# Row loads, pair loads and late statistics reordered in an attention and mixture-of-experts layer

## The chip, the core and the metric

The kernel runs on one NeuronCore of a Trainium2 chip. The metric is the device time of one execution, in microseconds; the medians below are over several executions. The core has five engines that run side by side, each with its own instruction queue: TensorE (PE, matmul), VectorE (DVE), ScalarE (ACT), GpSimd (POOL) and SyncE (SP), which here only issues DMA transfers. Semaphores tie them together: an engine that waits holds up everything behind the wait on its own queue.

## What is computed

One transformer layer on 4096 rows of 512 values, all float32:

```python
x = layernorm(x + attention(x))   # 8 heads of 128, window of 128, q and k normalised, gated
x = layernorm(x + ffn(x))
# ffn, for each row:
scores = softmax(x @ gate_w.T)             # 8 experts
weights, idx = top_k(scores, 2)
y = sum over the 2 chosen e of weights[e] * (silu(x @ w1[e].T) * (x @ w3[e].T)) @ w2[e].T
z = (silu(x @ ws1.T) * (x @ ws3.T)) @ ws2.T    # shared expert, every row
out = y + z
```

## The kernel before

Each float32 operand of a matmul is split into a high part and a low part (the rest), and a product is three matmuls: high by high, high by low, low by high. ScalarE makes the high parts, VectorE or GpSimd the low parts.

**First half, to about 1088 us.** 32 tiles of 128 rows go through projection, windowed attention, output projection, the first layer normalisation and the routing. A finished tile of rows is stored by `store_rows` in DRAM twice: in `x2_d`, from which the second half reads, and in `eo_d`, in which everything that a row gets later is added up. The routing writes a small record for each row and choice into the table `slot_d` (`scatter_records`, on POOL's queue).

**Second half.** `NQ` = 103 tiles (index q): 12 tiles of the shared expert on rows 0 to 1535 (`S1` = 12), 71 tiles of the eight experts on gathered rows (`NX` = 71), and 20 tiles of the shared expert on the remaining rows (`FIRST` = 83). Step q of TensorE transposes the rows of tile q+1 (L1135), transposes the product `gg` of tile q-1 (L1170), computes the hidden values of tile q (L1159) and the output of tile q-1 (L1187). Beside it ScalarE makes the high parts and the silu, VectorE the low parts (`split_b` L1474, `turned_low` L1751) and the product (`gate_hidden` L1742). TensorE can't compute an output before `gTl` of `turned_low` is there.

- *Early tiles.* SP's queue loads the rows of shared tiles q into five buffers (`bx`, `bx2`; `load` L491; a buffer is free when TensorE has transposed what it held) and the eight weight blocks of 1 MB (`weights` L487), in between. ScalarE and VectorE split one weight block in each of the steps 3 to 11. In step 9 (`SLOT_Q`) TensorE transposes the slot table (L1421), which POOL's queue reads (`slot_table`, L787) once all records have been scattered (L708). On POOL's queue the outputs of the early shared tiles are added into `eo_d` too (`z_store`, L767), partly ahead of the scatters.
- *Late tiles.* A pair of tiles of rows is combined as: sum of its two stored parts, `ga` and `gb` (loads L573 on SP's queue, the sum by POOL, L825), plus the output of the shared expert. For the pairs of early rows the latter is in `eo_d` already. For pair 6 (`EARLY`) the two outputs are kept in `zs` by ScalarE and added by POOL. For later pairs VectorE adds them out of the accumulator bank (`bank_total`, L1860), one tile per step. Then VectorE takes the statistics (`stats`, L1867 and L1869), POOL computes the factors (`pair_power`, L832 to L837), ScalarE normalises into `oo` (L1092) and SP stores. `ORDER` lists the pairs by the order in which they are combined and `AT` gives the step for each, counted from tile 83. Once the last expert result is in `eo_d`, SP loads six pairs at once, and later pair n+6 in the step of pair n; there are `NB` = 8 buffers. POOL adds pair n+3 in the step of pair n. The last pair is done on VectorE by itself (`finish_stats`, `finish_rows2`), and `finish_stats` waits for the factors of pair 14 (`fnm`).

## Time and profile before

| | us |
|---|---|
| median of 3 runs | 1606.99 |
| lowest, highest | 1604.16, 1607.1 |
| profiled execution | 1604.93 |
| its span | 1602.8 |

| engine | busy us | share |
|---|---|---|
| PE (TensorE matmul) | 1566.6 | 98% |
| DVE | 938.6 | 59% |
| ACT | 718.2 | 45% |
| POOL | 679.5 | 42% |

The engine rows of the page give the time in which an engine executed something. TensorE's share is an average: the places in which it stands idle, and those at which its granted clock is half, have to be looked up in its timeline. DMA carries little in the first half and is close to full from about 1090 us on.

### The profile page before, as it was taken

To read this page: it belongs to the slowest core of one execution; us is meant where nothing else is said; L and a number is where in the kernel's file an instruction comes from. 1 tells how busy PE (TensorE), PEld (TensorE's weight loads), DVE (VectorE), ACT (ScalarE), POOL (GpSimd) and SP (SyncE) were. 2 spreads that over 40 slices of the span, in tenths; PEclk is the share of its full clock that TensorE was granted. 3 is DMA by queue.
4 is the path that set the end of the run, shared out by engine and by line. 5 is a ranking of instruction groups with operands and counts; after the bars stand their busy time and mean duration, and the time that the engine had idled before them with its cause. 6 is when DMAs were issued, how large, how long until landed. Compare 5 with 4: busy or idle time off the path is not lost.

```text
span 1602.8 us, 31930 instructions
## 1 busy us (share of the span) xinstructions
PE 1566.6 (98%) x9650; PEld 1387.0 (87%) x9651; DVE 938.6 (59%) x2565; ACT 718.2 (45%) x1624; POOL 679.5 (42%) x636
## 2 busy tenths in 40 slices
PE   7999999999999999999999999999899999999898
PEld 6899999989999999989999999987778888888786
DVE  5555555655556555665565655657655555555376
ACT  4434333443334433443334333446455555655354
POOL 3323333243333432334324333253355555555375
PEclk9999999999999999999999999999999999999999
DMA  8111111111111111111112111139688888888993
GB/s 288 57 60 62 38 34 34 45 54 33 33 33 60 39 33 33 47 52 33 33 33 65 33 33 33 52 114 219 165 214 223 221 215 226 215 222 216 291 387 124
DMA packets 100960, 176.27 MB, mean 110 GB/s; under 512 B 11742, under 2 KB 28638, under 8 KB 100336
## 3 DMA queue, kind: packets, MB, share of 16 engines
q1 hardware_dynamic: 79360, 134.76, 24.9%
q0 software_dynamic: 20064, 40.86, 13.8%
q8 instruction: 26, 0.43, 0.1%
q10 hardware_dynamic: 1488, 0.04, 0.1%
q14 instruction: 22, 0.18, 0.0%
HBM read 128.04 MB, written 57.02 MB: 115 GB/s over the span
## 4 chain that ended last, share of the span: by engine, by line
PE 89%; DMA 6%; DVE 2%; issue 2%; POOL 1%; ACT 1%; SPq 0%; POOLq 0%; DVEq 0%; ACTq 0%
PE bank L1236 33%; PE bank L1159 14%; PE bank L1334 12%; PE bank L1311 7%; PE bank L1187 7%; PE bank L1285 6%; PE bank L1269 3%; PE bank L1298 3%; PE bank L1135 2%; DMA bx<-x_d 2%; DMA w_raw<-in_w2T 1%; PE bank L1170 1%; DMA passing<-in_wqkvT 1%; DMA gb<-eo_d 1%; DMA bx<-x_d,idxc 1%
## 5 line engine op out<-in xcount | busy, mean ns | idle before, releaser
L1236 PE MATMUL bank<-wh,xh 128*128 128x512 f32 (+2 forms) x896 | 339.1, 378 | 1.6 <-DVE wl L1450 1.5
L1236 PE MATMUL bank<-wl,xh 128*128 128x512 f32 (+2 forms) x896 | 327.6, 366 | 0.0
L1236 PE MATMUL bank<-wh,xl 128*128 128x512 f32 (+2 forms) x896 | 326.9, 365 | 0.0
L723 POOL TENSOR_TENSOR rnorm<-ssmax,nhalf 128x4 f32<-128x4 f32 x128 | 131.8, 1030 | 389.2 <-DVE ssmax L1488 383.9
L1236 PEld LDWEIGHTS bank<-wh,xh 128*128 128x128 f32 x896 | 170.2, 190 | 28.4 <-DVE wl L1450 2.1
L1236 PEld LDWEIGHTS bank<-wh,xl 128*128 128x128 f32 x896 | 170.0, 190 | 28.2
L1236 PEld LDWEIGHTS bank<-wl,xh 128*128 128x128 f32 x896 | 170.5, 190 | 22.3
L908 ACT ACTIVATE sq<-bank 128x512 f32<-128x512 f32 x128 | 75.7, 591 | 169.6 <-PE bank L1236 166.6
L1496 DVE TENSOR_TENSOR qkn<-bank,rnorm 128x512 f32<-128x512 f32 x128 | 88.4, 690 | 107.6 <-POOL rnorm L723 107.6
L1334 PE MATMUL bank<-woh,oh 128*128 128x256 f32 (+1 forms) x512 | 147.8, 289 | 1.0 <-DVE xr L1558 1.0
L1483 DVE TENSOR_REDUCE ssum<-sq 128x4 f32<-128x512 f32 x128 | 87.7, 685 | 103.7 <-ACT sq L908 95.9
L1334 PE MATMUL bank<-wol,oh 128*128 128x256 f32 (+1 forms) x512 | 145.0, 283 | 0.0
L1334 PE MATMUL bank<-woh,ol 128*128 128x256 f32 (+1 forms) x512 | 144.7, 283 | 0.0
L942 ACT ACTIVATE oh<-bank 128x512 fp32r<-128x512 f32 x64 | 38.2, 597 | 237.1 <-PE bank L1311 237.1
L917 ACT ACTIVATE qTh<-bank,qks 128x512 fp32r<-128x512 f32 x64 | 43.9, 686 | 211.6 <-PE bank L1269 211.6
L729 POOL TENSOR_TENSOR pp<-pp,gs 128x1024 f32<-128x1024 f32 x64 | 121.3, 1895 | 38.5 <-DVE gs L1541 38.5
L795 POOL DMA_INDIRECT bx<-x_d,idxc x71 | 81.3, 1145 | 124.2 <-DVE idxc L1845 92.6
L927 ACT ACTIVATE pp<-pp,neg_mx 128x256 f32<-128x256 f32 x256 | 126.8, 498 | 6.8 <-DVE neg_mx L1525 5.4
L1311 PEld LDWEIGHTS bank<-pT,vv 128*128 128x128 f32 x1024 | 122.1, 192 | 5.0 <-issue 2.3
L1311 PE MATMUL bank<-pT,vv 128*128 128x128 f32 x1024 | 124.8, 275 | 1.5 <-DVE wol L1714 1.3
L1546 DVE TENSOR_TENSOR ol<-bank,oh 128x512 fp32r<-128x512 f32 x64 | 44.3, 691 | 138.0 <-ACT oh L942 137.9
L1742 DVE TENSOR_TENSOR gg<-bank,gg 128x256 f32<-128x256 f32 x103 | 43.6, 424 | 127.0 <-ACT gg L1034 127.0
(225 smaller groups left out, 3869.2 us busy)
## 6 DMA issues: line engine op xcount, KB each, us to landing
w_raw<-in_w2T SPq DMA_DIRECT2D x71, 512.0 KB
eo_d<-zero_d SPq DMA_DIRECT2D x36, 256.0 KB, 3.0
xt<-in_xT SPq DMA_DIRECT2D x33, 256.0 KB, 3.2
xr<-in_x SPq DMA_DIRECT2D x32, 256.0 KB, 2.7
x_d<-xr SPq DMA_DIRECT2D x32, 256.0 KB, 2.1
eo_d<-xr SPq DMA_DIRECT2D x32, 256.0 KB, 2.3
w_f<-in_w13T SPq DMA_DIRECT2D x8, 1024.0 KB, 11.7
ga<-eo_d SPq DMA_DIRECT2D x16, 512.0 KB, 6.5
```

The lines of the kernel that those rows point to most:

```text
L723: pool.tensor_tensor(rnorm[:, :], ssmax[:, :], nhalf[:, :], ALU.pow).then_inc(rn_s, 1)
L729: pool.tensor_tensor(pp[:, g * HPG:(g + 1) * HPG, :], pp[:, g * HPG:(g + 1) * HPG, :], gs[:, g * HPG:(g + 1) * HPG].unsqueeze(2).to_broadc ...
L795: pool.indirect_dma_start(out=bx[:, b, :], out_offset=None, in_=x2_d, in_offset=bass.IndirectOffsetOnAxis(idxc[:, b, :], 0)).then_inc(bxg_ ...
L927: ins = act.activation(pp[:, h, :], pp[:, h, :], ACT.Exp, bias=neg_mx[:, h:h + 1], scale=-1.0, accum_out=esum[:, h:h + 1])
L1159: mm = pe.matmul(bank[2 + par][:, :], a[:, par, c, :], b[:, c, :], start=(c == 0 and k == 0), stop=(c == DC - 1 and k == 2))
L1187: mm = pe.matmul(bank[6 + par][:, :], a[:, par, m, :], b[:, m, :], start=(m == 0 and k == 0), stop=(m == IC - 1 and k == 2))
L1236: mm = pe.matmul(b[:, 0:n], a[:, par, c, :], wt[:, c, cols], start=(c == 0 and k == 0), stop=(c == DC - 1 and k == 2))
L1285: mm = pe.matmul(psS[b][:, hh * 2 * P:(hh + 1) * 2 * P], a[:, h, :], w[:, :, h, :], start=(k == 0), stop=(k == 2))
L1311: mm = pe.matmul(psO[:, hh * P:(hh + 1) * P], vv[:, k, g * HPG + hh, :], pT[:, hh, k * P:(k + 1) * P], start=(k == 0), stop=(k == 1))
L1334: mm = pe.matmul(out, a[:, h, :], b[:, h, cols], start=(h == 0 and k == 0), stop=(h == H - 1 and k == 2))
L1483: dve.tensor_reduce(ssum[:, :], sq[:, :].rearrange("p (h d) -> p h d", d=P), AX_X, ALU.add)\
L1496: dve.tensor_tensor(qkn[:, j, :].rearrange("p (h d) -> p h d", d=P), b[:, :].rearrange("p (h d) -> p h d", d=P), rnorm[:, :].unsqueeze(2). ...
```

## The change

- Row tiles 8 to 11 get a place of their own, `bx3`, where the low parts of the second weights will be written later. All of the rows 4 to 11 are loaded in one go when the output projection is done, before the last `store_rows`; the weight blocks 4 to 7 follow it. Load 3 goes ahead of the load of the second shared weights.
- `oo` has four buffers of finished pairs in place of two.
- The outputs of four late tiles, not two, are kept in `zs`; so pairs 6 and 7 are added by POOL and `bank_total` starts with tile 87, not 85. `ORDER` begins with pairs 0, 1, 8 and pair 7 comes late; the pairs are combined in the steps 5 to 20 behind tile 83, without a gap.
- SP loads four pairs at once, with the last two row fours among them, and then pair n+4 in the step of pair n; `NB` is 6.
- In the step of the last tile VectorE does `gate_hidden` before the pair's statistics.

```diff
-NB = 8
+NB = 6
-        zs = sbuf(s3, "zs", [P, 2, D])
+        zs = sbuf(s3, "zs", [P, 4, D])
-        oo = sbuf(s3, "oo", [P, 2, 2, D])
+        oo = sbuf(s3, "oo", [P, 4, 2, D])
...
+        s5 = ExitStack()
+        bx3 = sbuf(s5, "bx3", [P, 4, D])
+        s5.close()
...
-            if q0 >= FIRST + 2:
-                return bank_sum, q0 - FIRST - 1
+            if q0 >= FIRST + 4:
+                return bank_sum, q0 - FIRST - 3
...
-        ORDER = [0, 7, 1, 8, 2, 9, 3, 10, 4, 11, 5, 12, 6, 13, 14, 15]
-        AT = [4, 5, 6, 7, 8, 9, 10, 11, 12, 13, 14, 15, 16, 17, 19, 20]
-        FROM_BANK = EARLY + 1
+        ORDER = [0, 1, 8, 2, 9, 3, 10, 4, 11, 5, 12, 6, 13, 7, 14, 15]
+        AT = list(range(5, 21))
+        FROM_BANK = EARLY + 2
...
+            load(3, 3)
             sp.dma_start(sh2_raw[:, :, :], w2T[E, :, :].rearrange("(c p) n -> p c n", p=P)).then_inc(sh2_in, 16)
-            load(3, 3)
             store_rows(NT - 2, 0)
             weights(1)
             weights(2)
             weights(3)
-            store_rows(NT - 1, 1)
             sp.wait_ge(wo_s, 2 * NT)
             load(4, 4)
+            for q in (5, 6, 7):
+                sp.wait_ge(*place_free(q, q))
+                load(q, q)
+            for q in range(8, S1):
+                load(q, q)
+            store_rows(NT - 1, 1)
+            for e in range(4, E):
+                weights(e)
...
-                if n + 6 < PAIRS:
-                    load_pair(n + 6)
+                if n + 4 < PAIRS:
+                    load_pair(n + 4)
...
-                    for i in range(3):
+                    for i in range(2):
                         load_four(i)
...
-                    for n in range(6):
+                    for n in range(4):
                         load_pair(n)
-                        if n == 3:
-                            load_four(3)
+                        if n >= 2:
+                            load_four(n)
...
-                if ORDER[n] == EARLY:
+                if EARLY <= ORDER[n] < FROM_BANK:
...
-                    if n >= 2:
-                        act.wait_ge(o_out[n % 2], 32 * (n // 2))
+                    if n >= 4:
+                        act.wait_ge(o_out[n % 4], 32 * (n // 4))
...
-                if kind(q0 - 1) == "sh" and q0 - 1 < FIRST + 2:
+                if kind(q0 - 1) == "sh" and q0 - 1 < FIRST + 4:
                     take_shared(q - 1, q0 - 1)
...
+                if q0 == NQ - 1:
+                    gate_hidden(q, q0)
                 if pair_at(q0) is not None:
                     combine(pair_at(q0))
-                if q0 < NQ:
+                if q0 < NQ - 1:
                     gate_hidden(q, q0)
...
-                if FIRST + 2 <= q0 - 1 < NQ - 2:
+                if FIRST + 4 <= q0 - 1 < NQ - 2:
                     bank_total(q0 - 1)
```

## Rows read from the trace of the kernel before

**Rows 1.** TensorE's waits, 1060 to 1603: us in total, times, longest.
```profile
PE bank L1187 <- DVE gTl L1751: 6.9, 3, 5.6
PE bank L1135 <- DMA bx<-x_d: 5.5, 3, 3.1
```

**Rows 2.** TensorE's timeline, early tiles: start us, us, what [idle before, releaser].
```profile
1087.61 0.28 PE L1334 MATMUL bank<-woh,ol 128*128 128x256 f32 x1
...
1096.12 0.66 PE L1135 MATMUL bank<-ident,bx 128*128 128x128 f32 x4 [1.89 <-DMA bx<-x_d]
...
1126.42 0.66 PE L1135 MATMUL bank<-ident,bx 128*128 128x128 f32 x4 [3.06 <-DMA bx<-x_d]
...
1132.87 0.34 PE L1421 MATMUL bank<-ident,slot_t 71*128 71x71 f32 x2
1133.74 0.66 PE L1135 MATMUL bank<-ident,bx 128*128 128x128 f32 x4 [0.53 <-DMA bx<-x_d]
...
1138.58 0.60 PE L1135 MATMUL bank<-ident,bx 128*128 128x128 f32 x4
```

**Rows 3.** Timeline of SP's issuing queue, behind the last stores of rows.
```profile
1092.42 1.54 SPq L491 DMA_DIRECT2D bx<-x_d  x3
```

**Rows 4.** Chain of waits, in order of time, 1060 to 1200: start us, us, what.
```profile
1103.37 30.33 DMA bx<-x_d
```

**Rows 5.** Windows of 2 us: busy us by engine, granted clock, DMA share, GB/s.
```profile
1088.00:1090.00 2.00, 2.00 (x14) 1.74 (x13) 1.79 (x6) 1.25 (x3) 0.25 (x1) 1.00 0.07 28
...
1098.00:1100.00 2.00, 2.00 (x6) 1.52 (x6) 0.54 (x2) 1.98 (x2) 1.69 (x3) 0.50 0.83 314
```

**Rows 6.** POOL's timeline, early tiles: store with accumulation, last scatter, table read.
```profile
1101.11 1.06 POOL L767 DMA_DIRECT2D eo_d<-eo  x1
...
1107.54 0.96 POOL L708 DMA_INDIRECT slot_d<-rec_last,slot_last  x1 [0.30 <-issue]
...
1121.77 1.93 POOL L787 DMA_INDIRECT slot_t<-slot_d,blk_u  x1 [6.57 <-DMA slot_d<-rec_last,slot_last]
```

**Rows 7.** Line L767, accumulating stores of shared outputs: landing times.
```profile
DMA to landing us min/median/max: 4.2/10.8/18.6
```

**Rows 8.** TensorE's timeline, late tiles: the transposes of rows.
```profile
1505.38 0.60 PE L1135 MATMUL bank<-ident,xs 128*128 128x128 f32 x4
...
1510.13 0.60 PE L1135 MATMUL bank<-ident,xs 128*128 128x128 f32 x4
...
1521.99 1.05 PE L1135 MATMUL bank<-ident,xs 128*128 128x128 f32 x4
...
1527.43 0.60 PE L1135 MATMUL bank<-ident,xs 128*128 128x128 f32 x4
```

**Rows 9.** VectorE's timeline, the first sum out of a bank.
```profile
1517.58 0.69 DVE L1860 TENSOR_TENSOR ga<-bank,ga 128x512 f32<-128x512 f32 x1 [7.77 <-POOL ga L825]
```

**Rows 10.** POOL's timeline, second and third pair sum.
```profile
1515.20 2.34 POOL L825 TENSOR_TENSOR ga<-ga,gb 128x1024 f32<-128x1024 f32 x1 [0.25 <-DMA gb<-eo_d]
1517.89 2.35 POOL L825 TENSOR_TENSOR ga<-ga,gb 128x1024 f32<-128x1024 f32 x1 [0.34 <-DMA gb<-eo_d]
```

**Rows 11.** Waits of all engines, 1500 to 1603: ScalarE for the stores.
```profile
ACT oo L1092 <- DMA out<-oo: 2.4, 2, 1.7
```

**Rows 12.** Line L573, the pair loads: landing times.
```profile
DMA to landing us min/median/max: 4.5/7.8/13.1
```

**Rows 13.** VectorE's timeline, the last steps.
```profile
1590.91 0.69 DVE L1867 BATCH_NORM_STATS2 bn<-ga 128x6 f32<-128x512 f32 x1
...
1593.22 0.42 DVE L1742 TENSOR_TENSOR gg<-bank,gg 128x256 f32<-128x256 f32 x1 [0.45 <-ACT gg L1034]
...
1595.86 0.69 DVE L1867 BATCH_NORM_STATS2 bn<-ga 128x6 f32<-128x512 f32 x1
```

**Rows 14.** POOL's timeline, the factors of pair 14.
```profile
1592.86 0.23 POOL L832 TENSOR_SCALAR rs<-mv 128x2 f32<-128x2 f32 x1 [7.02 <-DVE mv L1869]
...
1594.26 0.20 POOL L837 TENSOR_TENSOR nm<-nm,rs 128x2 f32<-128x2 f32 x1
```

More of the change, by code:

```diff
@@ L343, in block_kernel @@
         o_s = sem("o_s")
-        o_out = [sem(f"o_out{i}") for i in range(2)]
+        o_out = [sem(f"o_out{i}") for i in range(4)]
         turns = {e.engine: sem(f"turns{n}") for n, e in enumerate((nc.sync, nc.gpsimd, nc.vector, nc.tensor))}
@@ L414, in place @@
         def place(q0):
+            if 8 <= q0 < S1:
+                return q0
             return (q0 + 2) % 4 if kind(q0) == "ex" else row(q0, q0) % 5 if q0 < FIRST + 4 else q0
@@ L422, in rows_of @@
                 return xs[:, q0 - FIRST - 4, :]
+            if 8 <= q0 < S1:
+                return bx3[:, q0 - 8, :]
             return bx[:, b, :] if b < 4 else bx2[:, b - 4, :]
@@ L429, in landed @@
             if q0 >= FIRST + 4:
-                return xs_in[(q0 - FIRST - 4) // 4], 16
-            return bx_in[place(q0)], 16 * (row(q, q0) // 5 + 1)
+                return xs_in[(q0 - FIRST - 4) // 4], 16 * (S1 - 8) + 16 if q0 >= FIRST + 16 else 16
+            if 8 <= q0 < S1:
+                return xs_in[3], 16 * (S1 - 8)
+            return bx_in[place(q0)], 16 * (sum(1 for p in range(q0 + 1) if place(p) == place(q0) and kind(p) == "sh"))
         def place_free(q, q0):
@@ L489, in load @@
             def load(q, q0):
-                sp.dma_start(rows_of(q0), x2_d[row(q, q0) * P:(row(q, q0) + 1) * P, :]).then_inc(bx_in[place(q0)], 16)
+                sp.dma_start(rows_of(q0), x2_d[row(q, q0) * P:(row(q, q0) + 1) * P, :])\
+                  .then_inc(xs_in[3] if 8 <= q0 < S1 else bx_in[place(q0)], 16)
             def store_rows(w, par):
@@ L587, in store_pair @@
                     sp.wait_ge(*((last_s, k + 1) if n == LAST else (o_s, 2 * n + k + 1)))
-                    sp.dma_start(out[(2 * c + k) * P:(2 * c + k + 1) * P, :], oo[:, n % 2, k, :]).then_inc(o_out[n % 2], 16)
+                    sp.dma_start(out[(2 * c + k) * P:(2 * c + k + 1) * P, :], oo[:, n % 4, k, :]).then_inc(o_out[n % 4], 16)
             def combine(n):
@@ L601, in step @@
                     load_second(q + 1, q0 + 1)
-                for k in ((5, 6) if q0 == 3 else (q0 + 3,)):
-                    if kind(k) == "sh" and k < FIRST + 4:
-                        sp.wait_ge(*place_free(k, k))
-                        load(k, k)
-                if 3 <= q0 < E - 1:
-                    weights(q0 + 1)
+                if FIRST <= q0 + 3 < FIRST + 4:
+                    sp.wait_ge(*place_free(q0 + 3, q0 + 3))
+                    load(q0 + 3, q0 + 3)
                 if q0 == FIRST:
                     sp.wait_ge(h_s, FIRST)
-                    for i in range(3):
+                    for i in range(2):
                         load_four(i)
@@ L624, in _ @@
             for q in o_out:
-                sp.wait_ge(q, 16 * NT // 2)
+                sp.wait_ge(q, 16 * NT // 4)
         @block.gpsimd
@@ L818, in add_pair @@
                 pool.wait_ge(g_in[b], 32 * (n // NB) + 32)
-                if ORDER[n] == EARLY:
+                if EARLY <= ORDER[n] < FROM_BANK:
+                    k = ORDER[n] - EARLY
                     pool.tensor_tensor(ga[:, b, :, :], ga[:, b, :, :], gb[:, b, :, :], ALU.add).then_inc(y_s, 1)
-                    pool.wait_ge(y_s, 1)
-                    pool.wait_ge(res_s2, S1 + 2)
-                    pool.tensor_tensor(ga[:, b, :, :], ga[:, b, :, :], zs[:, :, :], ALU.add).then_inc(gab_s, 1)
+                    pool.wait_ge(y_s, k + 1)
+                    pool.wait_ge(res_s2, S1 + 2 * k + 2)
+                    pool.tensor_tensor(ga[:, b, :, :], ga[:, b, :, :], zs[:, 2 * k:2 * k + 2, :], ALU.add).then_inc(gab_s, 1)
                     return
@@ L1089, in normalise @@
                 for k in range(2):
[L1090 to L1092 removed]
+                    if n >= 4:
+                        act.wait_ge(o_out[n % 4], 32 * (n // 4))
+                    act.activation(oo[:, n % 4, k, :], z_of(n)[:, k, :], ACT.Identity, bias=nm2[:, n % 2, k:k + 1],
                                    scale=rs2[:, n % 2, k:k + 1]).then_inc(o_s, 1)
@@ L1897, in finish_rows2 @@
                 if k == 0:
-                    dve.wait_ge(o_out[b], 32 * (LAST // 2))
-                dve.tensor_scalar(oo[:, b, k, :], z_of(LAST)[:, k, :], mv2[:, b, k, 0:1], rs2[:, b, k:k + 1],
+                    dve.wait_ge(o_out[LAST % 4], 32 * (LAST // 4))
+                dve.tensor_scalar(oo[:, LAST % 4, k, :], z_of(LAST)[:, k, :], mv2[:, b, k, 0:1], rs2[:, b, k:k + 1],
                                   ALU.subtract, ALU.mult).then_inc(last_s, 1)
```

1 line of the change is left out of this document (removed).

## Prediction

> **What bounds the kernel now.** I read the waits of TensorE first. Behind 1060 us, where the second half begins, TensorE waited mainly in two places: 6.9 us for `gTl`, 5.6 of it in one piece, and 5.5 us for rows in `bx`, 3.1 in the longest [rows 1]. Elsewhere it is busy end to end, so a change can only give back these stalls, and what the clock costs behind them. Reading order: waits, then TensorE's own timeline around each wait, then the engine or queue named as the releaser. Times are of the profiled execution (1604.93 us, its span 1602.8).
>
> The undisturbed step of a shared tile is 4.75 us, from transpose to transpose (1505.38 to 1510.13) [rows 8]. The stalls are read against it.
>
> **Early stretch, rows before weight blocks.** TensorE waits for row blocks at 1096.12 (1.89 us), at 1126.42 (3.06) and at 1133.74 (0.53) [rows 2]. The first wait has its cause in SP's order: row block 4 is issued only at 1092.42 [rows 3], behind the stores of the last 128 rows of `x2`, although TensorE's output projection ended at 1087.9 [rows 2]. DMA moved almost nothing from 1088 to 1090 (share 0.07) [rows 5]. The later waits come from SP's queue order: row block 10 was issued at 1103.37 and took 30.33 us, because it stood behind weight blocks [rows 4].
>
> After the change the blocks 4 to 11 are issued from about 1088.1, at some 0.5 us each (1.54 us for three [rows 3]), so until about 1092. The stores and the four weight blocks follow. At its landing time of 3.7 us (1096.12 less 1092.42) block 4 is there at 1091.8, before TensorE asks at 1094.23. So the wait of 1.89 us goes, and with it the half clock behind it: 0.50 in 1098 to 1100 [rows 5]. That is 12 matmuls in which about 1.4 us was lost; I take this from the clock row (some 3 us at half speed give up 1.5). The 3.06 and 0.53 us go too, since blocks 9 to 11 no longer stand behind weights. Counted alone, this is 1.89 + 1.4 + 3.06 + 1.4 + 0.53 = 8.3 us.
>
> **What is late next.** At step 9 TensorE also needs the slot table. Its transposes ran at 1132.87, 0.87 us before the late row block's [rows 2]. That table hangs on another chain, on POOL's queue: the store of tile 0 with accumulation at 1101.11, the last records scattered at 1107.54, the wait for them until 1121.77 (6.57 us of POOL idle), and the read of the table, which reached TensorE 11.1 us later [rows 2, 6]. Rows no longer hold TensorE, so it comes to step 9 at 1123.36 (1126.42 less 3.06) less 3.3, plus one step of 4.9 (4.84 is the one from 1133.74 to 1138.58 [rows 2]): about 1125. The table is not there then. What moves in its chain is little. The store at 1101.11 hangs on POOL's work before it, which the change doesn't touch; only the wait for the last slots, between the store's end at 1102.2 and the first scatter, shrinks, by about 1.2 us. DMA stays busy all the while. So the table comes at 1132.87 - 1.2 = 1131.7, and TensorE stands for some 6.5 us in one piece instead of 3.06 and 0.53. The half clock comes back behind that stall and costs 1.5. The next transposes then stand 0.34 us behind the table's, as they could have in the kernel before (1133.74 less 0.53 is 1133.21), at 1132.0, and the step behind is 4.84 + 1.5 long: 1138.35 against 1138.58. The early part thus gives back 0.2 us, by this sum; I take 0.5. Bounds: -1.1 (chain not earlier at all, clock loss paid) and +4 (chain earlier by the whole of the DMA time won, some 4.4 us between 1088 and 1092.4).
>
> The four late weight blocks stand behind two more row blocks (512 KB) and start up to 4 us earlier; they are wanted one per step until step 10, beyond 1135. The longest landing among the transfers in that queue is about 31 us, begun near 1100; so they are in time, price 0. The place ahead of the weights' low part is free until VectorE writes it in step 12: price 0.
>
> **The move of load 3 ahead of the second shared weights** swaps two neighbours in an idle queue: 0.
>
> **Late stretch: sums and statistics a step later.** The large stall: VectorE waits 7.77 us, until 1517.58, with tile 85's `bank_total` [rows 9], which needs the pair sum POOL began at 1515.20 [rows 10]. Behind it in VectorE's order stand the split and `gTl`, for which TensorE waits 5.6 us. From 1510.13 to 1521.99 it needs 11.86 us where 4.75 are due (7.11 lost), and the next step 5.44 (0.69 lost) [rows 8]; the second is the clock's tail. With some 0.3 us more in the steps behind, where a `gg` came late after ScalarE had waited for a store, that is 8.1 us.
>
> After the change the first `bank_total` is tile 87's. It falls due two steps behind 1510.13, so 9.5 us later, and some 0.3 us into that step: 1519.9. It needs three pair sums; the third began at 1517.89 and takes 2.35, so 1520.25 [rows 10]. It is 0.3 us late, and the result is wanted by TensorE only 3.4 us into the step, 1.1 us behind its usual time. So no stall here.
>
> The next demands: the queue delivers a pair (1 MB) per 2.69 us (1515.20 to 1517.89) [rows 10]. The order is now pairs 0, 1, 2, four row blocks (1 MB), pair 3, four row blocks, pair 4. Pair 4 thus lands at about 1517.8 + 4 x 2.6 = 1528.2, its sum is done at 1530.7, and tile 89's `bank_total` is due at 1529.4: 1.3 us late against 1.15 of slack. I price this at 0.2 us, and the ScalarE and POOL work pushed behind it at another 0.3, no more than ScalarE's late normalising cost in the kernel before. POOL does a pair in some 4 us (2.4 the sum [rows 10], 1.6 the power chain, 1592.86 to 1594.46 [rows 14]), so 0.75 us of each step is left to catch up. The second POOL sum of pairs 6 and 7 (2.4 us each, two steps apart) eats three steps of that; it comes when 1.2 us of slack is left at VectorE: 0.2 us.
>
> **Four buffers of finished rows** take away ScalarE's waits for stores, 2.4 us in two pieces [rows 11]. They are off the path apart from the few tenths counted above.
>
> **Four pairs ahead, six buffers.** A load for pair n+4 is issued about one step before POOL's step n+1, which wants it 10 us later; the median landing is 7.8 us, the longest 13.1 [rows 12]. In the closed loop (load, sum 2.4, power 1.5, normalise 1.5, store issue 1.1, waits 1) of four steps, 19 us, a landing of 11.5 us still fits. Price 0, bound 2.
>
> **The tail.** In step 102 VectorE now does `gate_hidden` (1593.22 to 1593.64) before the statistics of pair 14, which ran from 1590.91 to 1592.8 in the shadow of TensorE [rows 13]. They take 1.86 us and would now run until 1595.5. POOL's power chain followed them from 1592.86 to 1594.46 [rows 14], so it now ends at 1597.15. The last statistics wait for it (`fnm`): they began at 1595.86 [rows 13] and would begin at 1597.2. **Cost 1.3 us** on the path, nothing gained, since `gg` waited for ScalarE there anyway. The last `gTl` is some 0.7 us late too, beside the 1.3 and not added to it.
>
> **Sum.** 8.1 - 0.5 - 0.2 - 1.3 + 0.5 = 6.6 us. On the profiled execution's 1604.93 that is 1598.3; on the median of 1606.99 it is 1600.4. The runs shown spread by 3 us, so I take 1599.3.
>
> **Rivals.**
> 1. *The slot table's chain moves with the rows.* Speaking for it: DMA gets 4.4 us of work done that it did not before, and the table's read ran while SP's queue was still full. The accumulating stores on POOL's queue took up to 18.6 us to land when SP's queue was full and 4.2 at the least [rows 7]. If the queue empties 4 us earlier, the read and the stall end up to 4 us earlier: 1595.5. The Trainium skill, "DMA: Bandwidth & Descriptors", section "Queues, rings and completion order", says that each DMA engine takes turns between the queues that have work, packet by packet; by that rule POOL's transfers are slowed as long as SP's queue holds anything, which fits the two landing times and leaves it open whether the read is caught by the earlier end. Chance 0.2.
> 2. *The late stall isn't removed but halved.* The pair loads land later than in the old trace (two fours of row blocks now stand among them), POOL's sum for tile 89 comes 3 us or more late, and TensorE stands 2 to 3 us and pays 1.5 for the clock. Against: the pieces before pair 2 are unchanged. Time 1603.
>    Chance 0.15.
> 3. *Slower than before.* With six buffers a load waits for a normalised pair two steps back; if landings take 16 us in the steady part, the loop of four steps is 4.5 us too long, and over the ten later pairs (2.5 loops) 11 us are lost, against the 6.6: 1610. It decides from 11.5 us on, and turns the sum over at about 14.5. Longest seen 13.1, under a backlog that the change makes smaller. Chance 0.04.
> 4. *It doesn't do what it says:* the stalls go but return in full at the next wait (table early, pair 9 late): within 0.2%. Chance 0.06.
>
> **Chances.** Forecast 0.55, rivals 0.2, 0.15, 0.04, 0.06. A kernel of this kind can be told from no change beyond about 0.2%, or 3.2 us. Faster 0.84 (the forecast, rival 1, and 0.09 of rival 2, which lies near the edge), same 0.12 (the rest of rival 2, and rival 4), slower 0.04. The range reaches from rival 1's 1595.5, less 1.5 of spread, to rival 2's 1603: 1594 to 1603.5.
>
> **What would show it.** Early: no wait for `bx` rows up to step 12; one wait of 5 to 7 us ahead of the table's transposes; half clock behind it; SP's issues of `bx` in one block from 1088. If the wait ahead of the table is under 3 us, rival 1 holds. Late: no wait for `gTl` above 1 us; first `bank_total` near 1520; ScalarE without waits for stores. Tail: statistics of pair 14 behind the last `gg`, and 1.3 us more from the last `hidden` to the end. I am wrong if TensorE waits anywhere behind 1513 for more than 1.5 us.

## The result, and the profile after

The changed kernel takes 1599.78 us (median of 9 runs, 1597.22 to 1603.11) against 1606.99 of the kernel before (9 runs, 1604.16 to 1610.19). The ratio is 0.9963, with a 95% interval of 0.9953 to 0.9972: about 5.9 us faster, between 4.5 and 7.6. (The two medians lie 7.2 us apart; here and below a gain is read from the ratio.) The forecast was 1599.3, with a range of 1594 to 1603.5.

The profiled execution of the changed kernel took 1603.02 us (span 1601.2), among the slowest of its runs, while that of before (1604.93) is among the fastest of its own. So the two spans differ by only 1.6 us, and the traces have to be read by stretches. The table takes the start of TensorE's transposes of a tile's rows as marks. The stretch of the routed experts holds the same work in both kernels. The stretch from tile 12 to tile 18 (31.20 and 31.13 us) is left out.

| stretch, us | before | after | difference |
|---|---|---|---|
| tile 3 to tile 12 | 55.91 | 56.77 | +0.86 |
| tile 18 to tile 87, the experts | 330.33 | 334.01 | +3.68 |
| tile 87 to tile 102 | 79.48 | 71.29 | -8.19 |
| tile 102 to the end of the span | 17.94 | 20.06 | +2.12 |

Over all the kernels run here the expert stretch took between 329.2 and 334.0 us, whatever was changed around it, and no edit touches what is done in it. The 334.01 is the longest of all. Part of its 3.68 us can be read: behind a wait of 1.87 us for the rows of tile 18 the granted clock falls to 0.50, and the step takes 6.67 us; behind the 1.65 us of the kernel before it stays at 1.00, and the step takes 5.08. The fourteen traces of this document part at this place: the six with half clock there have 331.2 to 334.0 us for the stretch, the eight without 329.2 to 330.9. Leave the stretch out, and the rest sums to -5.2 us, which is near the 5.9 of the timed runs.

**TensorE's waits**, 1060 to 1603, after: us in total, times, longest.

```profile
PE bank L1436 <- DMA slot_t<-slot_d,blk_u: 6.5, 1, 6.5
PE bank L1185 <- DVE gg L1757: 3.2, 4, 1.6
PE bank L1150 <- DMA bx<-x_d,idxc: 2.2, 2, 1.9
PE bank L1202 <- DVE gTl L1766: 1.9, 2, 1.4
```

Both large waits of [rows 1] are gone: no wait for `bx<-x_d` is left and 1.9 us for `gTl`, of which 1.4 is in the very last product. In their place stands one wait of 6.5 us for the slot table, and four for `gg`, 3.2 us together, the longest 1.6.

**TensorE's timeline**, early tiles, after (answers to [rows 2]).

```profile
1094.07 0.60 PE L1150 MATMUL bank<-ident,bx 128*128 128x128 f32 x4
...
1101.38 0.44 PE L1185 MATMUL bank<-ident,gg 128*128 128x128 f32 x2 [1.57 <-DVE gg L1757]
...
1121.27 0.60 PE L1150 MATMUL bank<-ident,bx 128*128 128x128 f32 x4
1132.66 0.52 PE L1436 MATMUL bank<-ident,slot_t 71*128 71x71 f32 x2 [6.48 <-DMA slot_t<-slot_d,blk_u]
1132.97 1.06 PE L1150 MATMUL bank<-ident,bx 128*128 128x128 f32 x4
1139.42 0.60 PE L1150 MATMUL bank<-ident,bx 128*128 128x128 f32 x4
```

The rows are there whenever TensorE turns to them. It reaches the table at 1126.18 (1132.66 less 6.48) and stands. The step from 1132.97 to 1139.42 takes 6.45 us where the same step took 4.84 in [rows 2], so half clock costs 1.61 us here. Windows of 2 us show it (busy us by engine, granted clock, DMA share, GB/s): the granted clock is 0.50, TensorE's lower level of 1.2 GHz, until about 1136.

```profile
1130.00:1132.00 2.00, 0.00 (x0) 0.00 (x0) 0.00 (x0) 0.00 (x0) 0.00 (x0) 0.50 1.07 228
...
1134.00:1136.00 2.00, 2.00 (x8) 1.61 (x7) 1.83 (x8) 1.94 (x3) 0.00 (x0) 0.50 0.27 50
1136.00:1138.00 2.00, 2.00 (x9) 1.66 (x8) 1.35 (x2) 0.74 (x1) 0.00 (x0) 0.87 0.00 0
```

**SP's queue and POOL's timeline**, after (answer to [rows 3] and [rows 6]).

```profile
1087.92 3.67 SPq L500 DMA_DIRECT2D bx<-x_d  x8
...
1093.38 3.67 SPq L496 DMA_DIRECT2D w_f<-in_w13T  x4
```

```profile
1101.11 1.07 POOL L781 DMA_DIRECT2D eo_d<-eo  x1
...
1106.34 0.96 POOL L722 DMA_INDIRECT slot_d<-rec_last,slot_last  x1 [0.30 <-issue]
...
1123.47 1.91 POOL L801 DMA_INDIRECT slot_t<-slot_d,blk_u  x1 [10.23 <-DMA slot_d<-rec_last,slot_last]
```

The eight row blocks go out at 1087.92 and four weight blocks, 4 MB, at 1093.38, all at once. The last scatter of records was issued 1.2 us sooner than before, at 1106.34 against 1107.54, but the wait for it ended 1.7 us later, at 1123.47 against 1121.77. From that scatter to the read 17.1 us pass, against 14.2 before. This isn't yet a difference of the two kernels: the late part alone, which has the loads in their old order, takes 16.2 us (see the experiments).

**TensorE's and VectorE's timelines**, late tiles, after (answer to [rows 8] and [rows 9]).

```profile
1505.09 0.60 PE L1150 MATMUL bank<-ident,bx 128*128 128x128 f32 x4
...
1509.85 0.60 PE L1150 MATMUL bank<-ident,xs 128*128 128x128 f32 x4
...
1514.60 0.60 PE L1150 MATMUL bank<-ident,xs 128*128 128x128 f32 x4
...
1519.35 0.60 PE L1150 MATMUL bank<-ident,xs 128*128 128x128 f32 x4
```

```profile
1524.37 0.69 DVE L1875 TENSOR_TENSOR ga<-bank,ga 128x512 f32<-128x512 f32 x1 [0.59 <-PE bank L1202]
...
1529.13 0.69 DVE L1875 TENSOR_TENSOR ga<-bank,ga 128x512 f32<-128x512 f32 x1 [0.59 <-PE bank L1202]
```

Every step takes 4.75 us. Tile 87's transposes are at 1509.85 here and at 1505.38 in [rows 8], so the late part of this trace lies 4.47 us behind that of before. The first sum out of a bank waits 0.59 us for TensorE, where it waited 7.77 for POOL.

**The last steps**, after: VectorE (answer to [rows 13]), then POOL's factors (answer to [rows 14]).

```profile
1590.47 0.42 DVE L1757 TENSOR_TENSOR gg<-bank,gg 128x256 f32<-128x256 f32 x1 [2.29 <-ACT gg L1049]
1590.81 0.69 DVE L1882 BATCH_NORM_STATS2 bn<-ga 128x6 f32<-128x512 f32 x1
...
1594.43 0.70 DVE L1882 BATCH_NORM_STATS2 bn<-ga 128x6 f32<-128x512 f32 x1 [0.85 <-DVE ga L1875]
```

```profile
1592.75 0.23 POOL L847 TENSOR_SCALAR rs<-mv 128x2 f32<-128x2 f32 x1 [4.55 <-DVE mv L1884]
...
1594.14 0.19 POOL L852 TENSOR_TENSOR nm<-nm,rs 128x2 f32<-128x2 f32 x1
```

The statistics of pair 14 now stand behind the last `gg`; POOL's factors follow them and end at 1594.33, and the next statistics start at 1594.43. The releaser that the profile names for these, `ga L1875`, was done at 1593.58; the wait is POOL's.

### The profile page after: what moved, and what is told of

It reads as the page before. It is cut to its first block, busy times and chain, and to the rows that moved or that the text cites. A ratio compares the mean times of both kernels' runs of the same rounds, so it can differ in the third digit from the quotient of the medians.

```text
span 1601.2 us, 31929 instructions
## 1 busy us (share of the span) xinstructions
PE 1564.6 (98%) x9650; PEld 1384.2 (86%) x9651; DVE 938.9 (59%) x2563; ACT 720.6 (45%) x1626; POOL 680.9 (43%) x637
## 3 DMA queue, kind: packets, MB, share of 16 engines
q1 hardware_dynamic: 79360, 134.76, 25.3%
## 4 chain that ended last, share of the span: by engine, by line
PE 88%; DMA 5%; POOL 2%; DVE 2%; issue 2%; SPq 1%; ACT 1%; POOLq 0%; DVEq 0%; ACTq 0%
PE bank L1251 32%; PE bank L1174 14%; PE bank L1349 12%; PE bank L1326 7%; PE bank L1202 6%; PE bank L1300 6%; PE bank L1284 3%; PE bank L1313 3%; PE bank L1150 2%; DMA w_raw<-in_w2T 1%; PE bank L1185 1%; DMA passing<-in_wqkvT 1%; DMA slot_d<-rec_last,slot_last 1%; DMA slot_t<-slot_d,blk_u 1%; DMA bx<-x_d,idxc 1%
## 6 DMA issues: line engine op xcount, KB each, us to landing
w_f<-in_w13T SPq DMA_DIRECT2D x8, 1024.0 KB, 11.4
```

## Experiments

All ratios are to the kernel before, measured beside it. For runs of one group the interval is some 0.13% to each side, 2 us: the timed runs alone can't tell edits of 1 us apart, and where they can't, the stretches of the traces are used.

| kernel | ratio (95%) | tile 3 to 12 | tile 87 to 102 | to the end |
|---|---|---|---|---|
| before | 1 | 55.91 | 79.48 | 17.94 |
| after | 0.9963 (0.9953, 0.9972) | 56.77 | 71.29 | 20.06 |
| early part alone | 0.9994 (0.9985, 1.0003) | 54.46 | 78.22 | 18.02 |
| late part alone | 0.9961 (0.9947, 0.9974) | 56.10 | 71.30 | 18.97 |
| after, old order of the last step | 0.9956 (0.9943, 0.9970) | 57.33 | 71.31 | 18.96 |
| after, POOL's double sums apart | 0.9965 (0.9952, 0.9979) | 56.34 | 71.30 | 19.08 |
| after, records first | 0.9972 (0.9961, 0.9983) | 54.37 | 71.30 | 20.14 |
| after, two weight blocks held | 0.9958 (0.9945, 0.9971) | 55.55 | 71.30 | 20.11 |
| after, both of these | 0.9941 (0.9929, 0.9953) | 52.39 | 71.30 | 20.15 |
| after, all four edits | 0.9918 (0.9906, 0.9931) | 52.92 | 71.30 | 18.02 |
| after, stores behind the table | 0.9938 (0.9924, 0.9953) | 50.56 | 71.30 | 20.14 |
| the same, weights held | 0.9935 (0.9920, 0.9950) | 50.92 | 71.30 | 20.11 |
| stores behind, both tail edits | 0.9927 (0.9913, 0.9942) | 50.57 | 71.30 | 17.99 |
| the same, weights held | 0.9935 (0.9920, 0.9950) | 51.99 | 71.30 | 18.03 |

### The early part alone

The kernel before, with only the new place and the new order of loads; the late part is the old one.

```
+            if 8 <= q0 < S1:
+                return bx3[:, q0 - 8, :]
...
             load(4, 4)
+            for q in (5, 6, 7):
+                sp.wait_ge(*place_free(q, q))
+                load(q, q)
+            for q in range(8, S1):
+                load(q, q)
+            store_rows(NT - 1, 1)
+            for e in range(4, E):
+                weights(e)
```

> The kernel before with the early part of the change alone: rows 4 to 11 in one go, row tiles 8 to 11 in bx3, the last stores of x2 and weight blocks 4 to 7 behind them. My theory (the slot table's chain takes the place of the rows): no wait for rows, one wait of 5 to 7 us ahead of the table's transposes with the half clock behind it, so nothing is gained: ratio to the kernel before 0.999 to 1.001 (between 1.5 us faster and 1.5 us slower). Rival (rows before weights is a gain in itself, which the changed kernel's profiled execution lost elsewhere): 3 us or more faster, ratio 0.998 or less, and a wait under 3 us ahead of the table.

Measured: 1604.97 us (11 runs), ratio 0.9994 (0.9985 to 1.0003). All the waits for rows are gone, and TensorE's waits from 1086 to 1160 begin so:

```profile
PE bank L1435 <- DMA slot_t<-slot_d,blk_u: 4.2, 1, 4.2
PE bank L1184 <- DVE gg L1756: 1.6, 1, 1.6
```

So more than 5 us of waits for rows went, and the gain left of them is 1.0 us, between -0.5 and 2.4. The early part is close to nothing in time: the table, another chain on another queue, took the place of the rows. Its read was issued 15.9 us behind the last scatter. Of the traces above, four have this order of loads and no other early edit, and their stretch from tile 3 to 12 takes 54.46 to 57.33 us; two have the old order, with 55.91 and 56.10. No gain of the early part can be read from them either.

### The late part alone

The kernel before with the other parts of the change: four tiles in `zs`, four `oo`, the new `ORDER`, four pairs ahead. The early loads and the last step are as they were.

```
-        ORDER = [0, 7, 1, 8, 2, 9, 3, 10, 4, 11, 5, 12, 6, 13, 14, 15]
-        AT = [4, 5, 6, 7, 8, 9, 10, 11, 12, 13, 14, 15, 16, 17, 19, 20]
-        FROM_BANK = EARLY + 1
+        ORDER = [0, 1, 8, 2, 9, 3, 10, 4, 11, 5, 12, 6, 13, 7, 14, 15]
+        AT = list(range(5, 21))
+        FROM_BANK = EARLY + 2
...
-                if FIRST + 2 <= q0 - 1 < NQ - 2:
+                if FIRST + 4 <= q0 - 1 < NQ - 2:
                     bank_total(q0 - 1)
```

> The kernel before with the late part alone (sums out of a bank from tile 87, statistics a step later, four pairs ahead, six pair buffers, four buffers of finished rows), and gate_hidden behind the statistics in the last step, as before. My theory: the whole gain is here, 8.2 us from the transposes of tile 88 to those of tile 102, about 1 us lost again in step 101; 7.0 us faster, ratio 0.9955. Rival (both parts gain): 3 to 5 us faster, ratio 0.997 to 0.998.

Measured: 1598.32 us (5 runs), ratio 0.9961 (0.9947 to 0.9974), some 6.3 us. The 15 steps behind tile 87 take 71.30 us, as in the whole change. The end is 18.97 long, 1.0 more than before, although the last step has its old order: this 1.0 us belongs to the late part itself. Which of the late edits the 8 us hang on (the later first sum out of a bank, the order, the four buffers) was not tried one by one; that VectorE's wait for POOL is gone, the trace above shows. In the early part TensorE waits for rows again, 6.7 us in three pieces, the longest 5.1. The two parts taken together give 0.9955, which the whole change (0.9963) matches within its interval.

### The old order in the last step

From here on every edit is one of the changed kernel.

```
-                if q0 == NQ - 1:
-                    gate_hidden(q, q0)
                 if pair_at(q0) is not None:
                     combine(pair_at(q0))
-                if q0 < NQ - 1:
+                if q0 < NQ:
                     gate_hidden(q, q0)
```

> The changed kernel with the last step's order as before (statistics of pair 14 ahead of gate_hidden). My theory: the statistics go back into the shadow of TensorE's work, and 1.2 us of the end are given back: the time from the last transposes of rows to the end of the span is 18.9 us against 20.1; ratio to the kernel before 0.9955 where the changed kernel has 0.9963. Rival (in the new order the late gate_hidden of step 102 would be held up by the statistics, and that is why the end is not longer by the move): same or slower than the changed kernel, ratio 0.9963 or more.

Measured: 1598.03 us, ratio 0.9956 (0.9943 to 0.9970). In the trace the end is 1.10 us shorter (18.96 against 20.06), and 1.06 when the sums of the next edit are spread in both (18.02 against 19.08). The time agrees in sign, but its interval holds that of the change, so it is the trace that shows this one.

### POOL's double sums apart

Pairs 6 and 7 are each summed twice on POOL, 2.40 us a sum. In `ORDER` they come two steps apart and late; here they come in the eighth and twelfth place.

```
-        ORDER = [0, 1, 8, 2, 9, 3, 10, 4, 11, 5, 12, 6, 13, 7, 14, 15]
+        ORDER = [0, 1, 8, 2, 9, 3, 10, 6, 11, 4, 12, 7, 13, 5, 14, 15]
```

> The changed kernel with pairs 6 and 7 at places 7 and 11 of the order in place of 11 and 13, so that GpSimd's two additional sums lie four steps apart and end sooner. My theory: the 0.75 us wait for gg in step 101 and the 1 us that this step is long go, as GpSimd has caught up by then; 1.0 us faster than the changed kernel, ratio to the kernel before 0.9957. Rival (the loss in step 101 comes from DMA or ScalarE and not from GpSimd's backlog): the wait stays, ratio 0.9963.

Measured: 1598.98 us, ratio 0.9965 (0.9952 to 0.9979), no difference from the changed kernel that the timed runs could tell, and not the 0.9957 expected. In the trace the end is 0.98 us shorter. What goes is this chain in the changed kernel (timelines of POOL, ScalarE and TensorE):

```profile
1576.08 2.40 POOL L838 TENSOR_TENSOR ga<-ga,zs 128x1024 f32<-128x1024 f32 x1
```

```profile
1580.19 1.52 ACT L1107 ACTIVATE oo<-ga,nm,rs 128x512 f32<-128x512 f32 x2 [2.29 <-POOL nm L852]
```

```profile
1582.49 0.44 PE L1185 MATMUL bank<-ident,gg 128*128 128x128 f32 x2 [0.75 <-DVE gg L1757]
```

The second sum of pair 7 pushes POOL's factors back, ScalarE waits 2.29 us for them with the next `gg` behind, and TensorE stands 0.75 us. With the sums spread, the only wait of TensorE from 1560 on is the one of 1.43 us in the last product.

### What makes the slot table late

Three theories stood after this. Ahead of the last scatters on GpSimd's queue goes the accumulating store of tile 0; on SP's queue there are four weight blocks; or the scatter needs this time by itself. The first two edits take away one of the causes each, the third both.

`records_first`:

```
             table_constants()
-            z_store(0, 0)
             scatter_records(NG - 1, range(G))
+            z_store(0, 0)
             z_store(1, 1)
```

> The changed kernel with the last records' scatters ahead of the accumulating store of tile 0 on GpSimd's queue. Theory A (the records stand behind that store in GpSimd's queue, which takes 18.6 to 18.9 us to land): the records land 8 us or so earlier, the table's read is issued near 1114 instead of 1123.5, TensorE's wait ahead of it falls from 6.5 us to under 1, with the half clock behind it: 6 to 8 us faster than the changed kernel, ratio to the kernel before 0.9915 to 0.9925. Rival B (the records are slow because the DMA engines are shared with SP's weight blocks and row loads): the records go out 1.4 us earlier and land as long after as before; the wait falls to some 5 us, 1 to 1.5 us faster than the changed kernel, ratio 0.9955.

`weights_held`:

```
             for e in range(4, E):
+                if e == 6:
+                    sp.wait_ge(scat, 16 * NSC)
                 weights(e)
```

> The changed kernel with SP holding back weight blocks 6 and 7 (2 MB) until all records have landed. Theory A (the store of tile 0 ahead of them): little changes, wait ahead of the table 5 us or more, ratio to the kernel before 0.996. Rival B (the weight blocks' traffic): once blocks 4 and 5 are through, near 1106, the records have the engines to themselves and land before 1114; the table's read takes about 5 us beside 2 MB of weights or 9 at most; TensorE waits under 1 us, and 6 to 8 us are gained, ratio 0.9915 to 0.9925. If the held blocks come too late, TensorE waits at the first expert tile instead.

`both_table` has the two together.

> The changed kernel with both edits: records ahead of the store of tile 0, and weight blocks 6 and 7 held until the records have landed. Both theories: the wait ahead of the table is gone; 6.5 us of wait and 1.6 of half clock less what the next wait (the gathered rows of the first expert tile, 0.4 before) takes back: ratio to the kernel before 0.9915. If neither edit alone does it and this one does, the records need both.

Measured, with the chain in its two halves: from the issue of the last scatter to that of the table's read, from POOL's timelines, and from there to the table's transposes. Where TensorE doesn't wait, the second half is an upper bound.

| kernel | time, us | ratio | scatter to read | read to transposes | together | wait for the table |
|---|---|---|---|---|---|---|
| before | 1607.39 | 1 | 14.2 | at most 11.1 | at most 25.3 | none |
| after | 1599.78 | 0.9963 | 17.1 | 9.2 | 26.3 | 6.5 |
| early part alone | 1604.97 | 0.9994 | 15.9 | 8.2 | 24.1 | 4.2 |
| old order of the last step | 1598.03 | 0.9956 | 15.9 | 10.3 | 26.2 | 6.3 |
| double sums apart | 1598.98 | 0.9965 | 16.3 | 8.6 | 24.9 | 5.1 |
| records first | 1601.87 (10 runs) | 0.9972 | 12.8 | 11.4 | 24.2 | 3.9 |
| weights held | 1601.12 | 0.9958 | 13.3 | 10.8 | 24.1 | 4.3 |
| both | 1598.39 | 0.9941 | 11.0 | 11.0 | 22.1 | 1.9 |

The 1607.39 is of the kernel before beside the last three; the other rows had their own beside them, so times are compared by the ratio. The four kernels with the change's chain (rows two to five) show how far one execution lies from another: 15.9 to 17.1 us in the first half, 24.1 to 26.3 together. With the old order of loads the first half took 14.2 us in one trace and 16.2 in the other (the late part alone), so that the change made it longer is not shown.

Each edit takes 3 to 4 us off the first half, and neither the 6 to 8 that its theory wanted. The second half, 11.4 and 10.8 us, is longer than in any of those four and gives most of it back; why was not tried. The whole chain, 24.2 and 24.1 us, lies at the lower end of the four, and the waits for the table, 3.9 and 4.3 us, beside the 4.2 of the early part alone. The timed runs agree: 0.9972 and 0.9958 are no gain on 0.9963, and the first is worse than either of its theories expected. Only the two edits together shorten the whole chain clearly, to 22.1 us (22.7 in the kernel with all four edits). `both_table` is the first kernel that the timed runs set apart from the change (0.9929 to 0.9953 against 0.9953 to 0.9972, touching), at 0.9941 and not the 0.9915 expected. In all three the clock's loss stays: behind 3.90, 4.26 and 1.85 us of waiting the steps take 6.36, 7.47 and 6.41 us, where 4.84 are due.

```profile
1129.96 0.50 PE L1438 MATMUL bank<-ident,slot_t 71*128 71x71 f32 x2 [1.85 <-DMA slot_t<-slot_d,blk_u]
1130.25 1.06 PE L1152 MATMUL bank<-ident,bx 128*128 128x128 f32 x4
1136.66 0.60 PE L1152 MATMUL bank<-ident,bx 128*128 128x128 f32 x4
```

With both edits, a window of the 12 us from 1106 on shows what is left: the two weight blocks that were not held were issued by 1097.1 and took at most 13.2 us to land, the DMA engines are still nearly full, and yet they move little. Before it the same stretch of the change; the last two columns are DMA share and GB/s.

```profile
1106.00:1118.00 12.00, 11.41 (x58) 8.98 (x57) 11.39 (x24) 8.39 (x14) 4.61 (x6) 1.00 1.12 170
```

```profile
1106.00:1118.00 12.00, 11.12 (x55) 8.66 (x54) 10.86 (x25) 7.49 (x11) 6.86 (x8) 1.00 0.92 88
```

### All four edits

`both_table` with the old order of the last step and the spread sums, to see whether the pieces add.

> Both table edits, the old order in the last step, and pairs 6 and 7 spread. If the parts add up: 8 us of the table, 1.1 of the tail and 1.0 of step 101 on top of the changed kernel's 6: ratio to the kernel before 0.990; from the last transposes of rows to the end 17.9 us, as in the kernel before.

Measured: 1595.43 us (6 runs), ratio 0.9918 (0.9906 to 0.9931). The 0.990 expected lies outside that interval, because `both_table` had given less than expected; on top of its 0.9941 the 2.1 us of the two tail edits would make 0.9928, which lies within. So the pieces add: the end is 18.02 us long, as in the kernel before (17.94), and the early stretch 52.92. By the two ratios this is 0.9963 - 0.9918 = 0.0045, or 7 us, faster than the change.

### No store beside the records

The 0.92 with `both_table` raises the question of what fills the engines: the accumulating stores, which were only moved behind the scatters and run beside them, or the records. Here `z_store(0)` to `(3)` are issued behind the table's read.

```
             table_constants()
-            z_store(0, 0)
             scatter_records(NG - 1, range(G))
-            z_store(1, 1)
...
-                if q0 >= 4 and q0 - 2 < S1:
+                if q0 == 6:
+                    slot_table()
+                    for k in range(4):
+                        z_store(k, k)
+                if q0 >= 6 and q0 - 2 < S1:
+                    if q0 < 10:
+                        pool.wait_ge(*stored(q0 - 6, q0 - 6))
                     z_store(q0 - 2, q0 - 2)
...
-                if q0 == 6:
-                    slot_table()
```

> The changed kernel with all accumulating stores of tiles 0 to 4 issued behind the table's read on GpSimd's queue, the weight blocks as in the changed kernel. In the runs so far the table's read was issued 17.1 us behind the last record's scatter in the changed kernel, 12.8 with records ahead of the first store alone, 13.3 with weight blocks 6 and 7 held, 11.0 with both. Theory A (the accumulating stores, those behind the records too, hold the engines: DMA was full from 1106 to 1118 at 71 to 104 GB/s with both edits): 8 us or less, and TensorE's wait ahead of the table falls under 1 us. Theory B (the weight blocks): it stays at 12 us or more, with a wait of 3 to 4 us. Theory C (the records' own small packets): 10 us or more whatever else is moved, here and in the next kernel. Time, by A: 6 us faster than the changed kernel, ratio to the kernel before 0.9925; by B or C 0.9965.

The second kernel adds the wait of `weights_held`, so that neither queue has anything else.

> The same, with weight blocks 6 and 7 held back until the records have landed. Theory A: as the kernel before it in this row, 8 us or less. Theory B: 6 us or less, and clearly shorter than without the hold. Theory C (small packets): still 10 us or more with neither stores nor weights beside the records. Ratio to the kernel before 0.992 by A or B, 0.994 by C.

Measured: 1598.29 us, ratio 0.9938 (0.9924 to 0.9953), and 1598.03 us, ratio 0.9935 (0.9920 to 0.9950). Scatter to read is 12.6 and 8.5 us. TensorE never waits for the table, and both halves of the chain together are at most 20.2 and 20.1 us. In the second kernel DMA has little to do in the stretch read above, and from 1108 to 1112 next to nothing (its last scatter was issued at 1107.84):

```profile
1106.00:1118.00 12.00, 11.16 (x54) 8.67 (x54) 10.92 (x25) 7.48 (x11) 3.90 (x4) 1.00 0.18 29
1108.00:1112.00 4.00, 3.29 (x16) 2.44 (x14) 3.79 (x11) 3.16 (x5) 0.81 (x1) 1.00 0.03 5
```

So the high share with few GB/s went with the accumulating stores. The 8.5 us are the least that any kernel here took to the read (9.5 with both tail edits), and at least 4 of them are not time of the DMA engines, which stand at 0.03 there; what they are is open. With the weight blocks of SP beside the records it is 12.6 us. None of the three theories came out as written: without stores 8 us or less was wanted by the first, 12 or more with a wait of 3 to 4 us by the second, and without either 10 or more by the third.

The time did not follow by as much, and the timeline of TensorE shows one reason: the next thing it needs, the gathered rows of the first expert tile, is now late. In the first of the two kernels that again costs the clock.

```profile
1141.02 0.66 PE L1152 MATMUL bank<-ident,bx 128*128 128x128 f32 x4 [1.86 <-DMA bx<-x_d,idxc]
```

```profile
1142.00:1144.00 2.00, 2.00 (x6) 1.61 (x5) 1.66 (x3) 0.59 (x2) 0.65 (x1) 0.50 0.77 158
```

That step takes 6.42 us where the change has 4.81, but it begins with tile 12, so the table above doesn't hold the loss. In the second kernel the wait is longer, and nothing is lost behind it: the next step takes 4.81 us, and the granted clock is 1.00 in every window up to 1146.

```profile
1140.52 0.66 PE L1154 MATMUL bank<-ident,bx 128*128 128x128 f32 x4 [2.50 <-DMA bx<-x_d,idxc]
...
1145.33 0.60 PE L1154 MATMUL bank<-ident,bx 128*128 128x128 f32 x4
```

The early stretch is 50.6 and 50.9 us long, 6 less than in the change. Taken on to tile 18 it is 83.3 and 82.6 us against 87.9, so 4.6 and 5.3 less, which is what the timed runs give within their intervals (4.0 and 4.5).

### Stores behind, with both edits of the tail

> The stores behind the table's read, without the hold, with the old order in the last step and pairs 6 and 7 spread. The end costs 17.9 us from the last transposes of rows, 2.1 less than in the changed kernel; ratio 0.0013 below that of the stores alone.

> All edits together: stores behind, weights held, the old order in the last step, pairs spread. If the parts add up: 0.9905, the fastest of all.

Measured: 1596.15 us, ratio 0.9927 (0.9913 to 0.9942), and with the weights held 1598.31, ratio 0.9935 (0.9920 to 0.9950). The traces have the ends that were expected, 17.99 and 18.03. Holding the weights gives nothing here, neither in time nor in the early stretch (51.99 against 50.57); the 0.9905 expected was missed. It shortens the first half of the chain again, 9.5 us against 12.6, but not the whole: 21.1 us with a wait of 0.9, against at most 20.1 with none. The best of all are all four edits (0.9918) and the stores behind with both tail edits and no hold (0.9927), which can't be told apart; both are faster than the change and the kernel before.

## Why the prediction was right

The forecast was -6.6 us, 1599.3 after the choice between 1598.3 and 1600.4; the measured -5.9 lies beside it. The mechanism held in both parts; that the size came so near is in part luck, since several terms were off and offset each other. By its steps:

- **Rows before weights: right, and the size nearly.** It said that the three waits for rows go, that TensorE reaches the table at about 1125 and stands some 6.5 us, pays 1.5 for the clock, and that 0.5 us is left as a gain. The trace has 1126.18, 6.48 and 1.61; the profiled execution lost 0.86 us in this stretch, and the early part alone gained 1.0 us, with an interval from -0.5 to 2.4. The clock's term is not as fixed as one trace makes it look: of the seven other kernels that wait 1.9 to 6.3 us for the table, four lost 1.4 to 1.6 us there, but three lost 2.4 to 2.6 (steps of 7.22, 7.42 and 7.47 us behind waits of 6.31, 5.09 and 4.26). Two terms were off and offset each other. The stall begins 1.2 us later, mostly by a wait that the prediction did not have, 1.57 us for `gg` at 1101.38 (below). And the table came later: 1132.66 where 1131.7 was forecast.
- **The table's chain: one step failed.** "The wait for the last slots shrinks by about 1.2 us" was right for the issue of the last scatter, 1106.34 against 1107.54. That the read follows by the same amount was not: it was 1.7 us later, 17.1 us behind the scatter in place of 14.2. That the weight blocks which the change bunches did this is not shown, as the late part alone has 16.2 us with the old order. What failed is to take the time for the records to land as fixed: among executions with one order it differs by 1 to 2 us, and holding two weight blocks back takes 3.1 to 4.1 us off it when no store is beside it (12.6 to 8.5, 12.6 to 9.5). The prediction put the weight blocks at price 0 because they themselves are in time, and didn't ask what else has to land beside them.
- **The late stretch: right.** 8.1 us were expected and 8.19 are gone. The first `bank_total` was to fall due at 1519.9; it ran at 1524.37, which less the 4.47 us between the traces is 1519.90.
- **The losses around it: wrong by place.** The 0.3 and 0.2 us for the first sums did not come. The third pair sum ended at 1521.91, 2.5 us before it was wanted, and the fifth at 1532.75, 1.1 us before `bank_total` at 1533.88, where it was to be 1.3 late. The prediction left the pair loads where they were, relative to the steps. In fact they are issued 4.9 us behind the last scatter of the experts (1502.12 to 1506.99) and were 7.4 before (1497.65 to 1505.01). Only two fours of rows now stand ahead of that point of SP's queue, not three. The rows of SP's queue are

```profile
1494.38 0.98 SPq L597 DMA_DIRECT2D xs<-x_d  x2
1506.99 0.37 SPq L590 DMA_DIRECT2D ga<-eo_d  x1
```

  Whether the missing four is the cause was not tried by itself; the twelve kernels that load two fours have 4.6 to 5.9 us there, and the early part alone, with three, has 7.1.
- **POOL's double sums: under-sized.** Priced at 0.2 us, they cost 1.0 in the step of tile 102, by the kernel with the sums apart (19.08 against 20.06). The slack was counted at VectorE; the wait went through ScalarE, whose `gg` stands behind the late normalising.
- **Four `oo` buffers: right.** ScalarE's waits for stores, 2.4 us in [rows 11], are gone, and the 0.40 us of the step from 1536.93 to 1542.08 with them.
- **Six buffers, four pairs ahead: right, price 0.** Landings were 3.7, 6.3 and 13.2 us (lowest, median, highest), where [rows 12] has 4.5, 7.8 and 13.1; no sum of VectorE waited for POOL.
- **The tail: right in its chain.** 1.3 us expected, 1.1 measured with the order undone. The factors end 13.2 us behind tile 102's transposes (1594.33 less 1581.14), where they ended 9.6 behind them before (1594.46 less 1584.86, [rows 14]). Of these 3.6 us 1.0 is POOL's double sum, so 2.6 is the reordering, forecast at 2.7, and the last statistics waited for it as foreseen.

By these the sum is 8.19 - 1.0 - 1.1 + 1.0 (the early part alone) = 7.1, and with the 0.86 lost in the profiled execution instead, 5.2; the timed 5.9 lies between.

**The rivals.** The first said that the table comes up to 4 us earlier because SP's queue empties earlier. It falls: the wait for the table is 6.5 us, and 4.2 to 6.5 in the four kernels with the change's chain. That transfers of the two queues slow each other is so all the same: the records' 8.5 us become 12.6 with SP's weight blocks beside them. The rule that the rival named (the Trainium skill, "DMA: Bandwidth & Descriptors", section "Queues, rings and completion order": an engine takes turns between its queues, packet by packet) agrees with this. The second, a halved late stall, falls by the even steps of 4.75 us. The third, a loop of six buffers that is too short, by the landing times, 13.2 us at the most, and by the same even steps. The fourth has one half of truth: the early stalls did come back nearly in full at the next wait, but the late ones did not.

## What to carry to other kernels

A wait that is taken away is worth what the next need on the same engine leaves of it: look up when the next input arrives and which chain it hangs on, here a small scattered table on a queue of its own, before the gain is counted. Price a transfer that is moved or bunched not only by whether it is itself in time, but by what small transfers of other queues have to land beside it. Measure a chain to its end before an edit is called a gain: two edits took 3 to 4 us off the first half of this one, and the second half gave most of them back. And since even a stall of 1.9 us can cost 1.6 us of clock behind it, the gain is only whole when the stall is gone.

## What the runs showed of the hardware

**A tiny VectorE instruction of 1.87 us.** The conversion of four numbers for each of 128 rows took 0.17 us in the kernel before and 0.27 in the late part alone. In the changed kernel it took 1.87:

```profile
1098.79 0.17 DVE L1684 TENSOR_REDUCE slot_w<-work 128x2 f32<-128x16 f32 x1
1098.99 1.87 DVE L1685 CAST slot_last<-slot_w 128x4 uint32<-128x4 f32 x1
1100.90 0.42 DVE L1757 TENSOR_TENSOR gg<-bank,gg 128x256 f32<-128x256 f32 x1
```

At that time GpSimd is busy with hardly a pause:

```profile
1098.70 0.95 POOL L722 DMA_INDIRECT slot_d<-rec,slot_u  x1 [0.30 <-issue]
1099.66 1.15 POOL L700 IOTA jx<- 128x568 f32 x1
1100.74 0.15 POOL L702 MEMSET ones_e<- 128x8 f32 x1
```

It ends 0.05 us behind GpSimd's `IOTA` of 128x568 (1100.86 against 1100.81), and so it does in the early part alone and in the late part alone, where it began only 0.22 us before that end. The wait for `gg` (1.57 us, at full clock) is its consequence. The conversion took 1.82 to 1.90 us in all twelve kernels that have the early part in them. The Trainium skill, "Trainium Architecture — The Big Picture", section "What this means for kernel authors", says that VectorE and GpSimd share one pair of ports into SBUF as an exclusive lock, not a split of bandwidth. The rows agree with that, but no run moved the constants away, so the cause stays open.

**Share is not throughput.** DMA engines were 0.92 busy at 88 GB/s when small records and accumulating stores were nearly all that ran; in the kernel before, the late stretch from 1514 to 1540 has a share of 1.04 at 391 GB/s. A window's share alone doesn't say how much more would fit.

**The clock's price: not by the length of the stall, and not every time.** Behind 6.48 us of standing the next step was 1.61 us too long, behind 1.85 us it was 1.57 (6.41 less 4.84), behind 4.26 us 2.63 (7.47 less 4.84). Over all fourteen traces, behind 1090 us, the granted clock fell to 0.50 behind every stall of TensorE of 2.52 us or more. Of the seventeen between 1.83 and 2.50 us nine were followed by it and eight were not: it came behind 1.85 and 1.86 us, and not behind 2.41 and 2.50. Behind the stalls of 1.53 to 1.79 us, the 1.57 us for `gg` among them, the granted clock stayed at 1.00, and nothing was lost beyond the wait. What decides between the nine and the eight these rows don't show.
